# Two graph-attention layers in one kernel: the subtraction that forms the low half of the first layer's input, on GpSimd instead of VectorE from the eighth pair on

## The chip, the cores and the metric

One Trainium2 chip, one core of it. The metric is the device time of one execution in microseconds (us), the median over several runs. TensorE is called PE here, VectorE DVE, ScalarE ACT, GpSimd POOL, and SyncE, which issues all of the DMAs, SP. PEld is the loading of weights into PE, which overlaps the matmuls.

## The reference

The input is 64 graphs of 128 nodes with 256 features, `x` (64, 128, 256), and an integer adjacency `adj` (64, 128, 128). Two layers run one after the other.

```python
# layer 0
q, k, v = x @ Wq + bq, x @ Wk + bk, x @ Wv + bv        # 8 heads of 32
scores = einsum('bnhd,bmhd->bhnm', q, k) / sqrt(32); scores = where(adj == 0, -inf, scores)
h = einsum('bhnm,bmhd->bnhd', softmax(scores), v)
y = h @ Wo + bo + x;  x1 = layernorm(y) * gamma + beta
# layer 1, the same adj
q, k, v = x1 @ Wq.T + bq, ...;  p = softmax(where(adj == 0, -16384, q k^T)); z = v
for _ in range(4):
    z = 0.9 * (p @ z) + 0.1 * v
out = layernorm(x1 + z) * gamma + beta
```

## The kernel before, in words

The 64 graphs are worked on as 32 pairs. A pair's feature-major input is a tile of 128 partitions x 512 numbers (two chunks of 128 features, 2 x 128 nodes). The projections are made in three matmuls each instead of one: the input is split into a rounded copy `xh` and the rest `xl` (input minus rounded copy), the weights into `w_hi` and `w_lo`, and `xh·w_hi + xh·w_lo + xl·w_hi` is accumulated in PSUM (`project_T`, L338 to L345, and `project`, L347 to L353; the three products are `parts`, L324).

For the first layer the input comes by DMA into `xt_in` (two buffers, `load_xt`, L265). ACT rounds it into `xh[0]` (`split_hi`, L997; L1001), and DVE subtracts that from `xt_in` and writes `xl[0]` (`split_lo`, L1354; L1357). `xh[0]` and `xl[0]` have one buffer each. PE's `queries(0, ...)`, `keys(0, ...)` and `values(0, ...)` wait at their start for both counts, `xh_s` and `xl_s` (`x_ready`, L355 to L361), before the first of their matmuls, although `xl` is used only by the third product.

The order of the work is written out by hand. Each engine has its own list in three parts: `begin()` for the first pairs, `step(t)` for t = 7 to 31, and `end()`. A step works on many pairs at once, each at another stage. Engines run their lists strictly in order and meet at semaphores; a `Count` is a semaphore that rises by a fixed number per pair, so each wait names a pair.

What stands around the change in a step of each engine:

- DVE, `step` at L1688: the four `mask_scores(1, ...)` of pair t - 3, then `make_mask(t - 1)` (L1366), `split_lo(t)` (L1357), `save_ol(t - 2)` (L1423, which waits for ACT's `oh`), masked scores, `add_hop(1, ...)` (L1512), more masked scores, and `save_y(t - 2)` (L1439), the sum of the output projection and `xb`. At the step's head are `save_q(1)`, `add_hop(2, ...)` (L1512) and `reciprocals(0, 1, t - 2)` (L1409).
- POOL, `step` at L1981: `inverse_root(1, t - 8)` (L1872), `restart_term(t - 4)` (L1907, 0.1 v into `z0s`), `last_term(t - 4)` (L1914), `shift_residual(t - 3)` (L1899), `add_bias(t - 1)` (L1880, the row-major input plus a bias row, into `xb`; it waits for DVE's `save_y(t - 2)`), `inverse_root(0, t - 2)` (L1872), `probabilities` three times (L1859) with `scale_residual` (L1891) between them, `shift_out` (L1927), `scale_out` (L1921), and the last `probabilities`. `probabilities(0, 1, t - 1)` waits for DVE's reciprocals of that pair.
- PE, `step` at L671: for pair t - 1 it runs `queries(0, 0, t - 1)` (L699) behind the two `output` projections of pair t - 3, then values of the second layer, `queries(0, 1, t - 1)`, and so on. PE's step t + 1 is the one that uses what DVE's and POOL's step t make of pair t.
- SP, `step` at L312: `load_xt(t + 2)` waits for `xl_s` of pair t (L267), since the subtraction is the last reader of that `xt_in` buffer; then `store(t - 9)`, `load_x(t + 1)`, `load_adj(t + 2)`.

`begin()` on DVE holds `split_lo` of pairs 0 to 6; pairs 7 to 31 are split in `step`.

Of the kernel before, what the change touches and what calls it, by code (L numbers as in the profile page):

```python
# [6 lines left out]
FP32 = mybir.dt.float32  # L7
F32R = mybir.dt.float32r
I32 = mybir.dt.int32
ALU = mybir.AluOpType  # L10
# [69 lines left out]
def two_layers(nc, x, x_t, adj, w, rows, cols, ident_d, out):  # L80
    ctx = ExitStack()
    with ctx:
        def sb(name, shape, dt=FP32):
            return ctx.enter_context(nc.sbuf_tensor(name, shape, dt))
# [4 lines left out]
        def count(name, per=1):  # L89
            return Count(ctx.enter_context(nc.semaphore(name)), per)  # L90
# [30 lines left out]
        xt_in = [sb(f"xt_in{i}", [128, C, T]) for i in range(2)]  # L121
# [10 lines left out]
        xh = [sb(f"xh{l}", [128, C, T], F32R) for l in range(2)]  # L132
        xl = [sb(f"xl{l}", [128, C, T], F32R) for l in range(2)]
# [66 lines left out]
        xh_s = count("xh_saved")  # L200
        xl_s = count("xl_saved")
# [55 lines left out]
        def both(r):  # L257
            return r.broadcast_to([128, 2, D])
# [1075 lines left out]
        def _(dve):  # L1334
# [19 lines left out]
            def split_lo(p):  # L1354
                if p.real:
                    dve.wait_ge(xh_s.sem, xh_s.at(p))
                    nc.vector.tensor_tensor(xl[0][:, :, :], xt_in[p.parity][:, :, :], xh[0][:, :, :].bitcast(FP32),  # L1357
                                            ALU.subtract).then_inc(xl_s.sem, 1)
# [10 lines left out]
            def save_q(l, p):  # L1369
                if p.real:  # L1370
                    if p.is_(0):
                        dve.wait_ge(*((fold_s, 3) if l else (bq_s, 1)))
                    dve.wait_ge(qr[l].sem, qr[l].at(p))
                    dve.wait_ge(sr[l].sem, sr[l].at(p - 1))
                    raw = ps_q[l][:, :].rearrange("p (c t) -> p c t", c=C)
                    if l:
                        last = nc.vector.tensor_tensor(qT[l][:, :, :], raw, along(b1_col[:, 0, :]), ALU.add)
                    else:
                        last = nc.vector.scalar_tensor_tensor(out=qT[l][:, :, :], in0=raw, scalar=SCALE,
                                                              in1=along(bq0s[:, :]), op0=ALU.mult, op1=ALU.add)  # L1380
                    last.then_inc(q_s[l].sem, 1)

            def save_k(l, p):
                if p.real:
                    if l and p.is_(0):
                        dve.wait_ge(fold_s, 3)
                    dve.wait_ge(kr[l].sem, kr[l].at(p))
                    dve.wait_ge(sr[l].sem, sr[l].at(p - 1))
                    nc.vector.tensor_tensor(kT[l][:, :, :], ps_k[l][:, :].rearrange("p (c t) -> p c t", c=C),
                                            along(b1_col[:, 1, :] if l else col[:, BK0c, :]), ALU.add  # L1390
                                            ).then_inc(k_s[l].sem, 1)

            def mask_scores(l, b, c, p):
                if p.real:
                    dve.wait_ge(sr[l].sem, sr[l].at(p))
                    dve.wait_ge(mask_s.sem, mask_s.at(p))
                    dve.wait_ge(exps[l][b].sem, exps[l][b].at(p - 1))
                    for g in range(G):
                        h, o = G * c + g, 512 * g + (b * C + c) * N
                        last = nc.vector.tensor_tensor_reduce(  # L1400
                            sm[l][:, b, h, :], psS[:, o:o + N], mask[p.parity][:, b, :], -1.0, BIG,
                            ALU.add, ALU.min, nmax[l][:, b, h:h + 1])
                    last.then_inc(mx[l][b][c].sem, 1)

            def reciprocals(l, b, p):
                if p.real:
                    dve.wait_ge(exps[l][b].sem, exps[l][b].at(p))
                    dve.wait_ge(pr_s[l][b].sem, pr_s[l][b].at(p - 1))
                    nc.vector.reciprocal(rec[l][:, b, :], tot[l][:, b, :]).then_inc(rec_s[l][b].sem, 1)  # L1409
# [89 lines left out]
            def add_hop(j, p):  # L1499
                if p.real:  # L1500
                    dve.wait_ge(zr[j].sem, zr[j].at(p))
                    if j == NUM_HOP - 1:
                        dve.wait_ge(zf_s.sem, zf_s.at(p))
                        for used in on_s:
                            dve.wait_ge(used.sem, used.at(p - 2))
                        dst, add = y1[p.parity], zf[p.number % 4]
                    else:
                        if j == 0:
                            dve.wait_ge(z0_s.sem, z0_s.at(p))
                            dve.wait_ge(hr[NUM_HOP - 1].sem, hr[NUM_HOP - 1].at(p - 2))  # L1510
                        dst, add = z[p.parity], z0s[p.parity]
                    nc.vector.tensor_tensor(dst[:, :, :], ps_u[j][:, :].rearrange("p (b d) -> p b d", b=2), add[:, :, :],  # L1512
                                            ALU.add).then_inc(z_s[j].sem, 1)
# [174 lines left out]
            def step(t):  # L1688
                mask_scores(0, 1, 0, t - 2)
                save_q(1, t - 3)  # L1690
                add_hop(2, t - 6)
                reciprocals(0, 1, t - 2)
                save_k(1, t - 3)
                add_hop(0, t - 5)
                statistics(1, t - 7)
                mask_scores(1, 0, 0, t - 3)
                reciprocals(1, 1, t - 4)
                mask_scores(1, 1, 1, t - 3)
                mask_scores(1, 0, 1, t - 3)
                mask_scores(1, 1, 0, t - 3)  # L1700
                make_mask(t - 1)
                split_lo(t)
                save_ol(t - 2)
                mask_scores(0, 0, 1, t - 1)
                add_hop(1, t - 5)
                mask_scores(0, 0, 0, t - 1)
                save_y(t - 2)
                statistics(0, t - 2)
                aggregate(0, t - 2)
                save_q(0, t)  # L1710
                add_eps(0, t - 2)
                normalise(1, 0, t - 8)
                mask_scores(0, 1, 1, t - 1)
                normalise(0, 1, t - 2)
                normalise(0, 0, t - 2)
                reciprocals(1, 0, t - 3)
                normalise(1, 1, t - 8)
                save_k(0, t)
                aggregate(1, t - 7)
                add_hop(3, t - 6)  # L1720
                save_x1l(t - 2)
                save_hop(0, t - 4)
                reciprocals(0, 0, t - 1)
                add_eps(1, t - 7)
# [119 lines left out]

            begin()
            run(step, 7, PAIRS)
            end()

        @block.gpsimd
        def _(pool):  # L1850
# [12 lines left out]
            def inverse_root(l, p):  # L1863
                if p.real:
# [6 lines left out]
                            pool.wait_ge(used.sem, used.at(p - 1))  # L1871
                    nc.gpsimd.tensor_tensor(rstd[l][:, :], ve[l][:, :], mhalf[:, :], ALU.pow).then_inc(rstd_s[l].sem, 1)  # L1872

            def add_bias(p):
                if p.real:
                    if p.is_(0):
                        pool.wait_ge(fold_s, 1)
                    pool.wait_ge(x_s.sem(p), x_s.at(p))
                    pool.wait_ge(y_s.sem, y_s.at(p - 1))
                    nc.gpsimd.tensor_tensor(xb[:, :, :], x_in[p.parity][:, :, :], both(bo_row[:, :, :]), ALU.add  # L1880
                                            ).then_inc(xb_s.sem, 1)
# [12 lines left out]
            def shift_residual(p):  # L1894
                if p.real:
                    if p.is_(0):
                        pool.wait_ge(fold_s, 2)
                    pool.wait_ge(xg_s.sem, xg_s.at(p))
                    nc.gpsimd.tensor_tensor(zf[p.number % 4][:, :, :], zf[p.number % 4][:, :, :], both(r_row[:, :, :]), ALU.add  # L1899
                                            ).then_inc(xr_s.sem, 1)  # L1900
# [80 lines left out]
            def step(t):  # L1981
                inverse_root(1, t - 8)
                restart_term(t - 4)
                last_term(t - 4)
                shift_residual(t - 3)
                add_bias(t - 1)
                inverse_root(0, t - 2)
                probabilities(1, 0, t - 3)
                probabilities(0, 0, t - 1)
                scale_residual(t - 2)  # L1990
                probabilities(0, 1, t - 1)
                shift_out(t - 9)
                scale_out(t - 8)
                probabilities(1, 1, t - 3)
# [51 lines left out]

            begin()
            run(step, 7, PAIRS)
            end()

# [29 lines left out]
```

## Time and profile before

| what | us |
|---|---|
| median of 3 runs | 783.24 (782.63 to 788.65) |
| the profiled execution's own time | 786.14 |
| span of its trace | 784.0 |
| busy in the span: PE, PEld | 754.1, 710.6 |
| busy in the span: ACT, DVE, POOL | 665.7, 637.1, 547.8 |

The span runs from the first to the last instruction of the trace; the execution's own time has 2.1 us around it. From about 200 us to 659 us the trace repeats itself once per pair, every 22.96 us. A time in a row is the start from the beginning of the span; the next number is the duration. Consecutive instructions of one engine may overlap by a few hundredths of a us in the rows. In brackets stands how long the engine was idle just before and what ended that.

### The profile page before, as it was taken

What the parts mean: (1) busy time and instruction counts of PE and PEld (TensorE: products, weight loads), DVE (VectorE), ACT (ScalarE), POOL (GpSimd) and SP (SyncE); (2) the same over time, 40 slices, a digit from 0 to 9 for tenths busy, and PEclk for the clock granted to TensorE, in tenths of its full rate; (3) what the DMA queues carried; (4) which work ended last, traced back from release to release, by engine and by line L of the source; (5) the groups of instructions that cost most, each with busy time, mean ns of one, the idle gap of its engine ahead of it and who ended that gap; (6) DMA issues with size and microseconds to landing.
All of it is one profiled execution on the core that took longest, in us unless ns stands there. A gap on an engine that the chain in (4) does not pass through costs nothing.

```text
span 784.0 us, 32528 instructions
## 1 busy us (share of the span) xinstructions
PE 754.1 (96%) x11544; PEld 710.6 (91%) x11544; DVE 637.1 (81%) x3093; ACT 665.7 (85%) x2570; POOL 547.8 (70%) x417
## 2 busy tenths in 40 slices
PE   6889999999999999999999999999999999999974
PEld 6778999999999999999999999999999999998863
DVE  5778888888888888888888888888888888887765
ACT  4779998889889988988998898998889899899661
POOL 0336858666777777777787777787777778768774
PEclk9899999999999999999999999999999999999997
DMA  7101011010111101111111011111001111100002
GB/s 239 48 21 50 23 35 37 22 30 23 50 50 49 50 29 26 47 50 49 50 49 30 23 51 50 49 49 50 29 23 50 50 50 36 30 16 17 29 15 68
DMA packets 33245, 34.12 MB, mean 44 GB/s; under 512 B 2368, under 2 KB 28864, under 8 KB 33088
## 3 DMA queue, kind: packets, MB, share of 16 engines
q1 hardware_dynamic: 33088, 32.06, 13.8%
q8 instruction: 94, 1.54, 0.8%
q14 instruction: 63, 0.52, 0.2%
HBM read 23.67 MB, written 8.39 MB: 41 GB/s over the span
## 4 chain that ended last, share of the span: by engine, by line
PE 89%; DVE 3%; ACT 2%; issue 2%; DMA 1%; SPq 1%; POOL 1%; POOLq 0%; DVEq 0%; ACTq 0%
PE psF L342 23%; PE psF L411 18%; PE psF L351 16%; PE psF L401 15%; PE psS L391 9%; PE psF L456 7%; PE psF L436 2%; ACT ex L1011 2%; DMA w_raw<-in_w 1%; DVE sm L1400 1%; DMA out<-o_t 1%; SPq L284 0%; DVE o_t L1491 0%; DVE bst L1450 0%; POOL o_t L1927 0%
## 5 line engine op out<-in xcount | busy, mean ns | idle before, releaser
L1011 ACT ACTIVATE ex<-sm,nmax 128x128 f32<-128x128 f32 x1024 | 397.9, 397 | 3.3 <-DVE nmax L1400 2.3
L1859 POOL TENSOR_TENSOR pr<-ex,rec 128x1024 f32<-128x1024 f32 x128 | 245.3, 1918 | 101.1 <-DVE rec L1409 101.1
L1400 DVE CUSTOM_DVE_ANT_0 sm<-psS,mask 128x128 f32<-128x128 f32 x1024 | 228.3, 284 | 41.6 <-PE psS L391 41.4
L1011 ACT ACTIVATION_READ_ACCUMULATOR ex<-sm,nmax 128x1 f32 x1024 | 200.7, 196 | 0.0
L1022 ACT ACTIVATE pT<-psF 128x512 f32<-128x512 f32 x256 | 138.8, 596 | 34.5 <-PE psF L401 34.4
L401 PE MATMUL psF<-ident,pr 128*128 128x128 f32 x1024 | 137.8, 276 | 0.8 <-ACT pT L1022 0.5
L401 PEld LDWEIGHTS psF<-ident,pr 128*128 128x128 f32 x1024 | 112.7, 141 | 9.3 <-ACT pT L1022 0.9
L342 PE MATMUL psF<-xh,w_hi 128*128 128x256 f32 x512 | 112.6, 302 | 7.7 <-DVE w_lo L1339 5.7
L411 PE MATMUL psF<-pT,z 128*32 128x128 f32 x3072 | 103.1, 276 | 2.3 <-DVE z L1512 2.0
L342 PE MATMUL psF<-xh,w_lo 128*128 128x256 f32 x512 | 104.1, 285 | 0.0
L342 PE MATMUL psF<-xl,w_hi 128*128 128x256 f32 x512 | 103.6, 284 | 0.0
L342 PEld LDWEIGHTS psF<-xh,w_hi 128*128 128x128 f32 x512 | 79.8, 193 | 14.2 <-issue 12.6
L411 PEld LDWEIGHTS psF<-pT,z 128*32 128x32 f32 x3072 | 84.2, 111 | 8.1 <-issue 3.5
L1880 POOL TENSOR_TENSOR xb<-x_in,bo_row 128x512 f32<-128x512 f32 x32 | 41.7, 1302 | 70.2 <-DVE y L1439 52.9
L1400 DVE DVE_READ_ACCUMULATOR2_ANT nmax<- 128x1 f32 x1024 | 84.8, 83 | 0.0
L456 PE MATMUL psF<-ident,hT 128*128 128x128 f32 x512 | 76.4, 273 | 5.7 <-DVE hT L1416 3.9
L342 PEld LDWEIGHTS psF<-xh,w_lo 128*128 128x128 f32 x512 | 80.5, 193 | 0.0
L342 PEld LDWEIGHTS psF<-xl,w_hi 128*128 128x128 f32 x512 | 80.3, 192 | 0.0
L1872 POOL TENSOR_TENSOR rstd<-ve,mhalf 128x2 f32<-128x2 f32 x64 | 47.2, 737 | 43.5 <-DVE ve L1470 43.3
L391 PE MATMUL psS<-kT,qT 32*128 32x128 f32 x2048 | 75.3, 283 | 0.9 <-DVE nmax L1400 0.9
L391 PEld LDWEIGHTS psS<-kT,qT 32*128 32x128 f32 x2048 | 63.2, 186 | 11.8 <-issue 6.7
L1045 ACT ACTIVATE hT<-psF 128x512 f32<-128x512 f32 x96 | 57.0, 596 | 18.1 <-PE psF L411 18.0
(76 smaller groups left out, 1425.7 us busy)
## 6 DMA issues: line engine op xcount, KB each, us to landing
xt_in<-in_x_t SPq DMA_DIRECT2D x32, 256.0 KB, 3.0
x_in<-in_x SPq DMA_DIRECT2D x32, 256.0 KB, 3.0
out<-o_t SPq DMA_DIRECT2D x30, 256.0 KB, 2.2
adj_in<-in_adj SPq DMA_DIRECT2D x32, 128.0 KB, 2.4
pT<-in_w SPq DMA_DIRECT2D x4, 256.0 KB, 4.0
row<-in_rows SPq DMA_DIRECT2D x1, 768.0 KB, 6.8
w_raw<-in_w SPq DMA_DIRECT2D x3, 256.0 KB, 7.0
out<-o_t SPq DMA_DIRECT2D x4, 128.0 KB, 1.7
```

The lines of the kernel that those rows point to most:

```text
L342: last = nc.tensor.matmul(dst[:, c * T:(c + 1) * T], w_p[e][:, i, kc, c * 128:(c + 1) * 128], x_p[a][:, kc, :], start=(n == 0 and kc == 0) ...
L351: last = nc.tensor.matmul(dst[:, b * D:(b + 1) * D], x_p[a](kc), w_p[e][:, i, kc, :], start=(n == 0 and kc == 0), stop=(n == 2 and kc == C ...
L391: last = nc.tensor.matmul(psS[:, o:o + N], qT[l][r, c, b * N:(b + 1) * N], kT[l][r, c, b * N:(b + 1) * N], start=True, stop=True)
L401: last = nc.tensor.transpose(ps_T[l][b][c][:, g * N:(g + 1) * N], pr[l][:, b, G * c + g, :], ident[:, :])
L411: last = nc.tensor.matmul(dst[32 * g:32 * g + 32, o:o + N], src[:, b, h * HD:(h + 1) * HD], p_T[:, b, h, :], start=True, stop=True)
L456: last = nc.tensor.transpose(ps_u[j][:, o:o + 128], hT[p.parity][:, b * C + c, :], ident[:, :])
L1011: e = nc.scalar.activation(ex[l][:, b, h, :], sm[l][:, b, h, :], ACT.Exp, scale=-1.0, bias=nmax[l][:, b, h:h + 1], accum_out=tot[l][:, b, ...
L1022: nc.scalar.activation(pT[l][p.parity][:, b, G * c:G * c + G, :], ps_T[l][b][c][:, :].rearrange("p (g n) -> p g n", g=G), ACT.Copy).then_i ...
L1045: nc.scalar.activation(hT[p.parity][:, :, :], ps_h[j][:, :].rearrange("p (a n) -> p a n", n=N), ACT.Copy, scale=1.0 - ALPHA).then_inc(hT_s ...
L1400: last = nc.vector.tensor_tensor_reduce(sm[l][:, b, h, :], psS[:, o:o + N], mask[p.parity][:, b, :], -1.0, BIG, ALU.add, ALU.min, nmax[l][ ...
L1859: nc.gpsimd.tensor_tensor(pr[l][:, b, :, :], ex[l][:, b, :, :], rec[l][:, b, :].unsqueeze(2).broadcast_to([128, H, N]), ALU.mult).then_inc ...
L1872: nc.gpsimd.tensor_tensor(rstd[l][:, :], ve[l][:, :], mhalf[:, :], ALU.pow).then_inc(rstd_s[l].sem, 1)
```

## The change

From pair 7 on (the eighth), the subtraction `xt_in - xh` into `xl[0]` is no longer in DVE's step but in POOL's, between `shift_residual(t - 3)` and `add_bias(t - 1)`. Its operands, its shape, its waits and its count are the same; for pair 7 POOL also waits until DVE has done pair 6, so that the count stays in order. Pairs 0 to 6 stay on DVE. Nothing else is changed.

```diff
@@ DVE, step(t)
                 mask_scores(1, 0, 1, t - 3)
                 mask_scores(1, 1, 0, t - 3)
                 make_mask(t - 1)
-                split_lo(t)
                 save_ol(t - 2)
@@ POOL
+            def split_lo(p):
+                if p.real:
+                    pool.wait_ge(xh_s.sem, xh_s.at(p))
+                    if p.is_(7):
+                        pool.wait_ge(xl_s.sem, xl_s.at(p - 1))
+                    nc.gpsimd.tensor_tensor(xl[0][:, :, :], xt_in[p.parity][:, :, :], xh[0][:, :, :].bitcast(FP32),
+                                            ALU.subtract).then_inc(xl_s.sem, 1)
@@ POOL, step(t)
                 last_term(t - 4)
                 shift_residual(t - 3)
+                split_lo(t)
                 add_bias(t - 1)
                 inverse_root(0, t - 2)
```

## Rows read from the trace of the kernel before

**Rows 1.** The page, part 1: busy time, share of the span, instructions of each engine.
```profile
PE 754.1 (96%) x11544; PEld 710.6 (91%) x11544; DVE 637.1 (81%) x3093; ACT 665.7 (85%) x2570; POOL 547.8 (70%) x417
```

**Rows 2.** The page, part 4: the chain that ended last, shares by engine.
```profile
PE 89%; DVE 3%; ACT 2%; issue 2%; DMA 1%; SPq 1%; POOL 1%; POOLq 0%; DVEq 0%; ACTq 0%
```

**Rows 3.** Stretches of the span: length, busy time by engine, granted clock, DMA share, GB/s.
```profile
20.00:40.00 20.00, 16.80 (x162) 15.09 (x160) 15.80 (x58) 14.94 (x54) 8.07 (x6) 0.89 0.17 48
40.00:60.00 20.00, 18.07 (x212) 16.59 (x213) 14.13 (x83) 14.65 (x61) 7.04 (x6) 1.00 0.08 21
200.00:659.00 459.00, 459.00 (x7203) 437.48 (x7196) 384.50 (x1921) 411.02 (x1600) 344.44 (x261) 1.00 0.15 43
```

**Rows 4.** Timeline of DVE, pair 10: start us, duration us, engine, line, operation.
```profile
201.01 0.68 DVE L1357 TENSOR_TENSOR xl<-xt_in,xh 128x512 fp32r<-128x512 f32 x1
201.80 0.69 DVE L1423 TENSOR_TENSOR ol<-psF,oh 128x512 fp32r<-128x512 f32 x1
205.59 0.69 DVE L1439 TENSOR_TENSOR y<-psF,xb 128x512 f32<-128x512 f32 x1
```

**Rows 5.** Timeline of POOL, pair 10.
```profile
202.25 1.27 POOL L1914 TENSOR_TENSOR zf<-z0s,zf 128x512 f32<-128x512 f32 x1
203.49 1.28 POOL L1899 TENSOR_TENSOR zf<-zf,r_row 128x512 f32<-128x512 f32 x1
206.42 1.30 POOL L1880 TENSOR_TENSOR xb<-x_in,bo_row 128x512 f32<-128x512 f32 x1 [1.65 <-DVE y L1439]
```

**Rows 6.** Timeline of PE's weight loads: the first of queries(0, 0) for pair 10.
```profile
205.24 0.30 PEld L342 LDWEIGHTS psF<-xh,w_hi 128*128 128x128 f32 x2
```

**Rows 7.** Timeline of PE, DVE and POOL where POOL's next chain begins.
```profile
216.01 0.60 PE L456 MATMUL psF<-ident,hT 128*128 128x128 f32 x4
...
216.65 0.69 DVE L1512 TENSOR_TENSOR z<-psF,w_raw 128x512 f32<-128x512 f32 x1 [0.45 <-PE psF L456]
217.25 0.19 DVE L1409 RECIPROCAL rec<-tot 128x8 f32<-128x8 f32 x1
...
217.53 1.90 POOL L1859 TENSOR_TENSOR pr<-ex,rec 128x1024 f32<-128x1024 f32 x1 [0.26 <-DVE rec L1409]
```

**Rows 8.** Groups of POOL's instructions from 200 to 659 us: busy us, mean ns, idle before.
```profile
L1859 POOL TENSOR_TENSOR pr<-ex,rec 128x1024 f32<-128x1024 f32 x81 | 154.9, 1913 | 62.1 <-DVE rec L1409 62.1
L1907 POOL TENSOR_SCALAR z0s<-v 128x512 f32<-128x512 f32 x10 | 6.3, 632 | 0.8
```

**Rows 9.** Timeline of POOL, then of PEld: the same place for pair 30.
```profile
662.68 1.28 POOL L1899 TENSOR_TENSOR zf<-zf,r_row 128x512 f32<-128x512 f32 x1
...
664.44 0.30 PEld L342 LDWEIGHTS psF<-xh,w_hi 128*128 128x128 f32 x2
```

**Rows 10.** Timeline of POOL, DVE and PEld: the same place for pair 9.
```profile
178.66 1.59 POOL L1914 TENSOR_TENSOR zf<-w_raw,zf 128x512 f32<-128x512 f32 x1
180.21 1.29 POOL L1899 TENSOR_TENSOR zf<-zf,r_row 128x512 f32<-128x512 f32 x1
...
178.01 1.10 DVE L1357 TENSOR_TENSOR xl<-xt_in,xh 128x512 fp32r<-128x512 f32 x1
...
182.28 0.30 PEld L342 LDWEIGHTS psF<-xh,w_hi 128*128 128x128 f32 x2
```

**Rows 11.** Timeline of POOL and PEld: the same place for pair 7.
```profile
133.72 0.95 POOL L1907 TENSOR_SCALAR w_raw<-w_raw 128x512 f32<-128x512 f32 x1
135.99 1.31 POOL L1899 TENSOR_TENSOR zf<-zf,r_row 128x512 f32<-128x512 f32 x1
...
136.33 0.31 PEld L342 LDWEIGHTS psF<-xh,w_hi 128*128 128x128 f32 x2
```

**Rows 12.** Timeline of POOL and PEld: the same place for pair 31.
```profile
685.64 1.29 POOL L1899 TENSOR_TENSOR zf<-zf,r_row 128x512 f32<-128x512 f32 x1
...
688.84 0.30 PEld L342 LDWEIGHTS psF<-xh,w_hi 128*128 128x128 f32 x2
```

**Rows 13.** Timeline of SP's queue: the load of a later pair's input after pair 10's subtraction.
```profile
201.72 0.34 SPq L268 DMA_DIRECT2D xt_in<-in_x_t  x1
```

## The prediction

> **What bounds the kernel now.** I began with the page's busy shares. PE is busy 96% of the span, and even its weight loads fill 91%; ACT stands at 85%, DVE at 81%, POOL at 70% [rows 1]. The chain that ended last is PE to 89%, and POOL holds 1% of it [rows 2]. The table of stretches shows where the other 4% are: from 200 to 659 us PE is busy for 459.00 of 459.00 us at a granted clock of 1.00 of its 2.4 GHz level, so in the repeating part it waits for nobody, and the idle time lies in the opening and the ending [rows 3]. Two things follow. Work taken off DVE there can't shorten anything, because the engine that sets the period never waits for DVE. And whatever makes PE wait inside a period is added to that period in full, since PE has no gap in which to make it up. So the question is a single one: is the low half `xl` there when PE wants it? For that I laid the timelines of the four engines beside one another around one pair.
>
> **What is removed.** DVE's subtraction for pair 10 starts at 201.01 and takes 0.68, so `xl` is ready at 201.69 [rows 4]. PE's first weight load for that pair's queries is at 205.24 [rows 6]; the low half lies ready for 3.55 us. Taking 0.68 us off DVE brings DVE nothing: the next instruction, `ol`, starts at 201.80 and not at once, 0.11 us behind, because it waits for ACT's `oh` [rows 4], and at the head of the next step DVE waits 0.45 for PE before `z` [rows 7]. Gain: 0.
>
> **What is added.** One two-input instruction of 128x512 per pair on POOL, for pairs 7 to 31, 25 of them. The trace before has no such instruction on POOL with an fp32r output. Nearest rows: two inputs, the same shape, fp32 output, 1.27, 1.28 and 1.30 us [rows 5]. Bounds from further away: one input of that shape 0.632, two inputs of twice the size 1.913 [rows 8]. I take 1.28, the row of the same shape that sees the same neighbours. On DVE it was 0.68, so it is 0.60 longer; but that isn't the cost. The cost is where POOL's order puts it.
>
> POOL comes to it only after `shift_residual`, which starts at 203.49 and ends at 204.77 [rows 5]. POOL's instructions overlap by 0.03 (202.25 + 1.27 against 203.49), so the subtraction starts at 204.74 and ends at 206.02. PE must then be told. DVE to POOL takes 0.14 (`y` ends at 206.28, `xb` starts at 206.42 [rows 4, 5]) or 0.09 (`rec` ends at 217.44, `pr` starts at 217.53 [rows 7]); no row shows POOL to PE, so I take 0.10 and keep 0.05 to 0.20. `xl` counts for PE from 206.12, and PE wanted it at 205.24 [rows 6]. The queries wait for both halves before their first product, so no work in front covers this: **0.88 us of PE stall**.
>
> **Is the stall there in every period?** Only if POOL's chain does not come earlier as seen from PE once PE is late. The chain runs without a gap from `probabilities(0, 1)`. That one waited 0.26 for DVE's `rec`, which directly follows `z`, and `z` waited 0.45 for PE's transposes at 216.01 [rows 7]. Those transposes stand behind the queries in PE's list. So a late PE makes a late POOL chain, and the next pair finds the same 0.88. The period becomes 22.96 + 0.88 = 23.84. Pair 30 has the same distances as pair 10: `shift_residual` ends at 663.96, PE loads at 664.44, 0.48 later, against 205.24 - 204.77 = 0.47 [rows 5, 6, 9]. Pairs 10 to 30 are 21: 21 x 0.88 = **18.5**.
>
> **The first pairs and the last.** For pair 9 `shift_residual` ends at 181.50 and PE loads at 182.28, 0.78 later [rows 10]; pair 8 has the same distance. DVE's subtraction took 1.10 there and POOL's `last_term` beside it 1.59, against 0.68 and 1.27 for pair 10 [rows 4, 5, 10]. That collision goes with the change, so POOL is 0.32 earlier: `shift_residual` ends at 181.18, the subtraction at 181.18 - 0.03 + 1.28 = 182.43, and with 0.10 that is 182.53, a stall of 0.25; two pairs: **0.5**. Pair 7: `shift_residual` ends at 137.30, less 0.32 because `z0s`, which took 0.95 beside DVE's subtraction, goes back to 0.63: 136.98. The subtraction ends at 138.23, counts at 138.33, and PE wanted it at 136.33: **2.0** [rows 11]. Pair 31: `shift_residual` ends at 686.93, so `xl` counts at 688.28, and PE loads only at 688.84 [rows 12]: **0**.
>
> The collisions bear on a rule. The Trainium skill (SBUF — State Buffer, section "SBUF: two separate sides") says that DVE and POOL share a pair of ports as a lock, held for a whole instruction, and that a DVE instruction with two inputs in SBUF contends with a POOL one that reads SBUF. The trace agrees for pair 9 (1.10 and 1.59). By that rule alone the change takes away DVE's only such instruction of the repeating part, which speaks for it; but from pair 10 on DVE's 0.68 and POOL's 1.27 show nothing to win back, and the rule changes the sum by the 0.32 us already counted for the first pairs.
>
> **What moves on the queues.** `add_bias` stands behind the new instruction. It waits for `y`, ready at 206.28, and POOL is free at 206.02, so it still starts at 206.42: the 1.65 us in which POOL idled there hold the 1.28 [rows 5]. SP issues the next load into this `xt_in` buffer at 201.72 on DVE's count [rows 13], and will at about 206.1, 4.4 us later; that load is for two pairs on, two periods of 22.96 away, and nothing else of SP's becomes due before. Cost: 0. If that cover were gone it would be at most the 4.4 us once.
>
> **Sum.** 18.5 + 0.5 + 2.0 + 0 = 21.0 us. The profiled execution has 784.0 of span and 2.1 around it, 786.14, and would become 807.1. The median is 783.24, so I forecast 783.24 + 21.0 = **804.2**. Its own range: with 1.27 and 0.05 a period loses 0.82, 21 x 0.82 + 2.1 = 19.3; with 1.33 and 0.20 it loses 1.03, 21.6 + 2.6 = 24.2. With a microsecond for the medians: 801.5 to 808.5.
>
> **Rivals.**
>
> *Not slower: POOL's chain comes earlier.* If what releases POOL's `probabilities(0, 1)` were DVE's own work and not PE, then DVE, lighter by 0.68, and standing idle more while PE stalls, would hand over `rec` earlier as seen from PE, and the stall would die out after a pair or two. It decides at 0.88 us: that much earlier and nothing is lost, 783.2 to 785. For it: DVE is at 84% in the repeating part (384.50 of 459.00 [rows 3]). Against it: the 0.45 of waiting for PE right in front of `rec` [rows 7]. Chance 0.04. The Trainium skill (Perfetto Trace Analysis, section "Identifying the Most-Contended Engine") has the most occupied engine set the pace; by that alone an instruction moved between DVE and POOL, neither of them the fullest, leaves 783.2. It says nothing of order, and the 0.47 us between POOL and PE is a matter of order.
>
> *A cheap subtraction.* If POOL did it at the one-input price, 0.632, the stall would be 0.88 - 0.65 = 0.23 and pairs 8 and 9 would have none: 21 x 0.23 + 1.4 = 6.2, so 789.4, within 1% of before. Against it: every two-input row of this shape is at 1.27 or more. Chance 0.05.
>
> *A dear subtraction.* If the fp32r output or a collision brought it to the 1.913 of the double size, each of 24 stalls grows by 0.63: 21.0 + 24 x 0.63 = 36.1, so 819.3. A collision is possible: DVE runs `y`, with `xb` in SBUF and the other input in PSUM, from 205.59 [rows 4], inside the new instruction. Against it: no POOL row of the repeating part is stretched beside such DVE work. Chance 0.09.
>
> *The clock falls.* The granted clock was 0.89 from 20 to 40 us, where PE was busy 16.80 of 20, but 1.00 from 40 to 60 with 18.07 of 20 [rows 3]. The new period has PE idle for 0.88 of 23.84, 4%, far less than the 10% that kept 1.00. If it did fall to 0.89, the 522 us from 160 to 682 would take 65 us more, about 869. Chance 0.02.
>
> **How the numbers follow.** Forecast 0.80, dear 0.09, cheap 0.05, not slower 0.04, clock 0.02. Predicted 804.2. The range 797 to 812 holds the forecast's own and reaches half-way to the cheap and the dear case. One per cent, 7.8 us, is about what a measurement of this kernel can tell from no change. Within it lie the cheap case and nearly all of the not slower one: 0.08; faster by more than 1% 0.01, since PE has next to nothing to win; slower 0.91.
>
> **What would show it.** Right: POOL's `xl` of about 1.28 us directly behind `shift_residual`; PEld L342 now idle 0.6 to 1.0 us per pair, released by POOL's `xl`, about 20 us in all; a period of 23.8 us; `xb` still released by `y`; DVE's waits for PE longer; pair 7's stall near 2 us and pair 31's none; a granted clock of 1.00. Wrong: a period of 22.96 and no wait of PE on POOL; POOL's `probabilities(0, 1)` no longer waiting for `rec`; the new instruction far from 1.28; or PE waiting elsewhere in the period, on ACT or DVE.

## The result, and the profile after

| | before | changed |
|---|---|---|
| median of 4 runs each, us | 784.11 (782.63 to 788.65) | 805.43 (803.18 to 809.84) |
| the profiled execution, own time | 786.14 | 806.28 |
| its span | 784.0 | 803.7 |

The ratio is 1.0278, 95% interval 1.025 to 1.0307: 2.8% slower. The forecast was 804.2.

The page of the changed kernel, part 1 (busy time and shares, as in [rows 1]) and part 4 (the chain that ended last, as in [rows 2]):

```profile
PE 758.3 (94%) x11544; PEld 710.7 (88%) x11544; DVE 619.9 (77%) x3068; ACT 665.1 (83%) x2570; POOL 577.8 (72%) x442
...
PE 35%; POOL 34%; issue 22%; ACT 4%; DVE 3%; DMA 1%; POOLq 1%; SPq 0%; DVEq 0%; ACTq 0%
```

DVE is lighter by 17 us, POOL heavier by 30, and none of the engines is anywhere near full except PE. Yet POOL, which held 1% of the chain, holds 34%: it now leads from `rec` through POOL's instructions to `xl`, and from there through PE back to `rec`. That is the picture of an engine that is idle for more than a quarter of the time and nevertheless on the path.

The same place in the timelines as in [rows 5, 6], for pair 10 of the changed kernel; first POOL, then PE's weight loads:

```profile
203.55 1.27 POOL L1921 TENSOR_TENSOR zf<-z0s,zf 128x512 f32<-128x512 f32 x1
204.78 1.28 POOL L1906 TENSOR_TENSOR zf<-zf,r_row 128x512 f32<-128x512 f32 x1
206.03 1.28 POOL L1878 TENSOR_TENSOR xl<-xt_in,xh 128x512 fp32r<-128x512 f32 x1
207.73 1.30 POOL L1887 TENSOR_TENSOR xb<-x_in,bo_row 128x512 f32<-128x512 f32 x1 [0.42 <-DVE y L1439]
```
```profile
206.31 0.31 PEld L351 LDWEIGHTS psF<-w_hi,ol 128*128 128x128 f32 x2
207.42 0.30 PEld L342 LDWEIGHTS psF<-xh,w_hi 128*128 128x128 f32 x2 [0.81 <-issue]
...
207.46 0.47 PE L342 MATMUL psF<-xh,w_hi 128*128 128x256 f32 x2 [0.63 <-POOL xl L1878]
```

`xl` takes 1.28 and ends at 207.31, and PE's next weight load starts 0.11 later. It had been idle for 0.81. The bracket of the weight load names "issue", which is the profile's word for time in which it sees no wait; the matmul that follows names the releaser, POOL's `xl`. It does so for 22 of the 25 pairs: pair 7 and pairs 10 to 30. `xb` is still released by `y`; its idle time shrank from 1.65 to 0.42, so the added instruction did fit where POOL had been idle.

The head of POOL's next chain, against [rows 7], DVE and then POOL:

```profile
218.83 0.69 DVE L1512 TENSOR_TENSOR z<-psF,w_raw 128x512 f32<-128x512 f32 x1 [0.45 <-PE psF L456]
219.44 0.19 DVE L1409 RECIPROCAL rec<-tot 128x8 f32<-128x8 f32 x1
...
219.71 1.90 POOL L1858 TENSOR_TENSOR pr<-ex,rec 128x1024 f32<-128x1024 f32 x1 [0.26 <-DVE rec L1409]
```

The two waits, 0.45 and 0.26, are what they were to the hundredth. PE's delay travels through DVE into POOL, and the next pair meets the same stall. What DVE gave up became waiting: per pair it waits 0.7 for ACT's `oh` in front of `ol` (0.1 before), and 1.2 for PE's `queries(0, 0)` and `queries(0, 1)` in front of their `qT` (0.3 before). The first weight loads of `queries(0, 0)` of pairs 10 and 30 are at 207.42 and 684.72: 477.30 / 20 = 23.87 us per pair, against 22.96.

Here is where the time went, from the first weight load of `queries(0, 0)` of each pair in the two traces:

| from pair to pair | before, us | changed, us | more |
|---|---|---|---|
| 6 to 7 | 23.10 | 25.09 | 1.99 |
| 7 to 8 | 22.99 | 24.73 | 1.74 |
| 8 to 9 | 22.96 | 23.22 | 0.26 |
| 9 to 30 | 482.16 | 501.14 | 18.98 |
| 30 to 31 | 24.40 | 24.42 | 0.02 |
| together | 575.61 | 598.60 | 22.99 |

The spans differ by only 19.7, because the changed kernel's opening, up to pair 6, was 2.7 us shorter in its trace, and the ending 0.6. The opening isn't touched by the change: the profiled execution of before had a granted clock of 0.89 from 20 to 40 us [rows 3], and that of the changed kernel had 1.00. The experiments' traces have either, whatever the kernel (figures in the last section). The medians of several runs average over this, though with four runs each only roughly, and they say 21.3.

One line of that table isn't explained by a stall: from pair 7 to pair 8 PE waited for `xl` only 0.27 us (its weight loads idle for 0.19, and the usual overlap of 0.08 lost). The table of stretches of the changed kernel, columns as in [rows 3], shows the rest:

```profile
134.00:136.00 2.00, 0.34 (x3) 0.37 (x4) 1.57 (x5) 2.00 (x11) 2.00 (x3) 0.98 0.00 0
136.00:138.00 2.00, 2.00 (x12) 2.00 (x11) 0.00 (x0) 0.14 (x2) 0.76 (x1) 0.50 0.53 133
138.00:140.00 2.00, 2.00 (x14) 2.00 (x14) 0.42 (x1) 0.00 (x0) 0.00 (x0) 0.66 0.38 130
140.00:144.00 4.00, 4.00 (x43) 3.83 (x45) 2.97 (x17) 2.90 (x9) 2.60 (x2) 1.00 0.02 4
...
206.00:683.00 477.00, 464.19 (x7199) 439.15 (x7199) 372.45 (x1901) 410.79 (x1599) 369.05 (x281) 1.00 0.14 41
```

Right after pair 7's wait (PE busy 0.34 of 2 us) the granted clock is 0.50 and then 0.66 of 2.4 GHz. That is the 1.2 GHz level for all of the one stretch and two thirds of the other, some 3.4 us. PE's first matmul behind the wait, two rows inside that time and two behind it, each of two matmuls:

```profile
135.66 0.53 PE L342 MATMUL psF<-xh,w_hi 128*128 128x256 f32 x2 [1.85 <-POOL xl L1878]
...
136.42 0.63 PE L342 MATMUL psF<-xl,w_hi 128*128 128x256 f32 x2
136.84 0.63 PE L351 MATMUL psF<-w_hi,xh 128*128 128x256 f32 x2
...
139.38 0.40 PE L351 MATMUL psF<-w_hi,xh 128*128 128x256 f32 x2
139.62 0.40 PE L351 MATMUL psF<-w_lo,xh 128*128 128x256 f32 x2
```

Two take 0.43 from start to start there (0.42 in these two rows), and 0.24 at the full clock; over 3.4 us that is a loss of 3.4 x (1 - 0.24 / 0.43) = 1.5. With pair 8's own stall of 0.27 it gives the 1.74 of the table. The stalls of 0.9 us from pair 10 on are followed by nothing of the kind: 1.00 throughout. This is one profiled execution. Of the other three of the changed kernel one, the 803.18, had a mean granted clock of 0.994 against the 0.992 of this one, so the fall may not come in every execution; no trace shows one without it.

### The profile page after: what moved, and what is told of

Same layout as the page of the kernel before. It is cut to its first block, busy times and chain, and to the rows that moved or that the text cites. A ratio compares the mean times of both kernels' runs of the same rounds, so it can differ in the third digit from the quotient of the medians.

```text
span 803.7 us, 32529 instructions
## 1 busy us (share of the span) xinstructions
PE 758.3 (94%) x11544; PEld 710.7 (88%) x11544; DVE 619.9 (77%) x3068; ACT 665.1 (83%) x2570; POOL 577.8 (72%) x442
## 4 chain that ended last, share of the span: by engine, by line
PE 35%; POOL 34%; issue 22%; ACT 4%; DVE 3%; DMA 1%; POOLq 1%; SPq 0%; DVEq 0%; ACTq 0%
POOL pr L1858 11%; PE psF L342 11%; PE psF L351 8%; PE psF L401 6%; PE psF L411 5%; POOL zf L1921 4%; POOL o_t L1934 4%; POOL zf L1898 4%; POOL zf L1906 4%; POOL xl L1878 3%; PE psS L391 2%; ACT ex L1011 2%; POOL rstd L1871 2%; PE psF L456 2%; POOL o_t L1928 1%
```

## The experiments

The intervals are those of the ratio to the kernel before, which was run again beside each group of experiments (medians 783.15 to 784.09). "Period" is the time from pair to pair between 200 and 660 us in the profile.

| kernel | median, us | ratio | period, us |
|---|---|---|---|
| changed | 805.43 | 1.0278 (1.025 to 1.0307) | 23.87 |
| xl one place earlier on POOL | 784.47 | 1.0003 (0.998 to 1.0026) | 22.96 |
| xl at the head of POOL's step | 782.65 | 0.9982 (0.9958 to 1.0005) | 22.96 |
| xl behind xb on POOL | 923.83 | 1.1789 (1.1751 to 1.1827) | 28.0 to 29.5 |
| extra work on POOL | 783.87 | 0.9994 (0.9971 to 1.0018) | 22.96 |
| no low half | 781.96 | 0.9975 (0.9957 to 0.9993) | 22.96 |
| PE waits at the third product | 792.74 | 1.0119 (1.0088 to 1.015) | 23.33 |
| POOL from pair 9 | 801.93 | 1.0232 (1.0202 to 1.0262) | 23.85 |
| late on DVE | 813.40 | 1.0383 (1.0341 to 1.0425) | 24.13 |
| PE's values first | 787.77 | 1.0032 (1.0006 to 1.0058) | 23.08 |

### The place in POOL's list: one earlier, three earlier, one later

```diff
 # POOL, step(t), from the changed kernel: one place earlier
                 last_term(t - 4)
+                split_lo(t)
                 shift_residual(t - 3)
-                split_lo(t)
                 add_bias(t - 1)
```

> The subtraction stays on POOL but stands one place earlier, in front of shift_residual instead of behind it. Theory A (place): the price is only how late xl is for PE. xl then ends about 1.25 us earlier, near 204.8 on the scale of pair 10, and PE wants it at 205.24, so no stall from pair 8 on and some 0.7 us once for pair 7: 784.5 to 786, a period of 22.96. Rival B (load): an engine of which 1.3 us per pair more is asked, or POOL being the slower engine for it, costs the time wherever it stands: 803 to 806.

It came out at 784.47, not distinguishable from before. POOL and PEld for pair 10:

```profile
203.41 1.30 POOL L1878 TENSOR_TENSOR xl<-xt_in,xh 128x512 fp32r<-128x512 f32 x1
204.66 1.31 POOL L1906 TENSOR_TENSOR zf<-zf,r_row 128x512 f32<-128x512 f32 x1
...
205.17 0.30 PEld L342 LDWEIGHTS psF<-xh,w_hi 128*128 128x128 f32 x2
```

`xl` ends at 204.71, 0.46 before PE loads, and nobody waits. Two neighbouring lines exchanged in one engine's list are worth 21 us. Pair 7 still stalled once, by 0.8 (23.87 from pair 6, against 23.10).

```diff
 # POOL, step(t), from the changed kernel: at the head
                 inverse_root(1, t - 8)
+                split_lo(t)
                 restart_term(t - 4)
                 last_term(t - 4)
                 shift_residual(t - 3)
-                split_lo(t)
                 add_bias(t - 1)
```

> The subtraction on POOL stands directly behind inverse_root(1), in front of restart_term. A: xl ends near 202.8, 2.4 us before PE wants it; shift_residual ends near 206.05, still before xb's wait for y ends at 206.42. No stall, pair 7 included: 783.5 to 785. B: 803 to 806. A third outcome, 786 to 790, would mean that the terms now 1.3 us later (z0s, last_term) are missed by DVE's last hop.

782.65: a little below the forecast, its interval holds 1. POOL and PEld for pair 10:

```profile
198.64 1.28 POOL L1878 TENSOR_TENSOR xl<-xt_in,xh 128x512 fp32r<-128x512 f32 x1
...
202.46 0.30 PEld L342 LDWEIGHTS psF<-xh,w_hi 128*128 128x128 f32 x2
```

`xl` ends at 199.92 and PE loads at 202.46; pair 7 has no stall either (22.99). `z0s`, `last_term` and `shift_residual`, each 1.3 us later, are missed by nobody.

```diff
 # POOL, step(t), from the changed kernel: behind add_bias
                 shift_residual(t - 3)
-                split_lo(t)
                 add_bias(t - 1)
+                split_lo(t)
```

> The subtraction on POOL stands behind add_bias instead of in front of it. A: xb ends at 207.72, xl at 208.97, PE gets it at about 209.1, 3.9 us after 205.24: 24 x 3.9 + 3 for pair 31 = 97, so 881 if the granted clock stays at 1.00. If each stall of that length is followed by 3.4 us at half clock, as the one of 2.03 us of pair 7 was, 1.7 us more per pair: about 922. B: 803 to 806.

923.83, near the larger of theory A's two figures. POOL, PEld for pair 10, and the stretch from 206 to 659 us (columns as in [rows 3]):

```profile
220.67 1.27 POOL L1887 TENSOR_TENSOR xb<-x_in,bo_row 128x512 f32<-128x512 f32 x1 [1.66 <-DVE y L1439]
221.90 1.26 POOL L1878 TENSOR_TENSOR xl<-xt_in,xh 128x512 fp32r<-128x512 f32 x1
...
223.28 0.50 PEld L342 LDWEIGHTS psF<-xh,w_hi 128*128 128x128 f32 x2 [3.72 <-issue]
...
206.00:659.00 453.00, 396.34 (x5662) 376.61 (x5661) 293.19 (x1499) 324.17 (x1263) 291.63 (x223) 0.91 0.12 35
```

PE stood still for 3.72 us in every pair. Those stalls would make a period of 22.96 + 3.8 = 26.8; the mean from pair 7 to pair 30 is (796.58 - 137.71) / 23 = 28.65. The 1.9 us beyond it are the clock: 0.91 on average where it was 1.00, and the weight load behind the wait takes 0.50 for two where it took 0.30. Once per period the trace has a stretch at the 1.2 GHz level, of 3.4 or 6.8 us. From the first weight load of pair 7 to that of pair 30 these add up to 109.3 us, of which 10.4 lie inside the waits and cost nothing more. The other 98.9 are 4.3 per pair, and at the rate of the changed kernel 4.3 x (1 - 0.24 / 0.43) = 1.9. That the 922 was met so closely is partly luck: it was worked out with 3.4 us per pair at half speed, 1.7.

### Is it the load, or the engine?

```diff
 # from the kernel before: DVE keeps its subtraction, POOL does one more, for t = 7 to 31
                 shift_residual(t - 3)
+                extra(t)      # scratch = row[:, 0:2, :] - row[:, 2:4, :], 128x512, fp32r
                 add_bias(t - 1)
```

> DVE keeps its subtraction as in the kernel before; POOL does an additional one of the same shape from constant tiles into a tile that nobody reads, at the place of the change, pairs 7 to 31. A: it fits into the 1.65 us in which POOL waits for y, nobody waits for it: 783.5 to 785.5, period 22.96. B (POOL's 1.3 us of additional work is what costs): 803 to 806.

783.87. POOL's rows at that place:

```profile
202.22 1.31 POOL L1879 TENSOR_TENSOR scratch<-row 128x512 fp32r<-128x512 f32 x1
203.91 1.30 POOL L1888 TENSOR_TENSOR xb<-x_in,bo_row 128x512 f32<-128x512 f32 x1 [0.38 <-DVE y L1441]
```

The same instruction at the same place, with nobody waiting for it, is free. Work on POOL is not what costs.

```diff
 # from the kernel before, DVE, step(t)
                 make_mask(t - 1)
-                split_lo(t)
                 save_ol(t - 2)
                 mask_scores(0, 0, 1, t - 1)
                 add_hop(1, t - 5)
                 mask_scores(0, 0, 0, t - 1)
+                split_lo(t)
                 save_y(t - 2)
```

> The subtraction stays on DVE but stands directly in front of save_y instead of in front of save_ol. A (only lateness counts, not the engine): it would end at 206.27 on the scale of pair 10, PE gets it 1.1 us after 205.24, period 24.1, 24 pairs x 1.1 = 26: 809 to 813. Rival D (it is the move to POOL that costs, by the slower engine or the shared ports): 783 to 786.

813.40, slower than the changed kernel, although nothing moved to POOL and the subtraction took 0.69. DVE and PEld for pair 10:

```profile
206.56 0.69 DVE L1357 TENSOR_TENSOR xl<-xt_in,xh 128x512 fp32r<-128x512 f32 x1
...
207.36 0.30 PEld L342 LDWEIGHTS psF<-xh,w_hi 128*128 128x128 f32 x2 [1.08 <-issue]
```

On the faster engine, but done later, it costs more: the period is 24.13, 1.17 over before. The median is 0.4 above the top of what was expected; the period grew by 1.17 and not by 1.1, which makes 24 x 0.07 = 1.7. With that, and with the two places on POOL that cost nothing, the rival that blames the engine or the shared ports is out.

### What could have been won

```diff
 # from the kernel before: no split_lo from pair 7 on
 # DVE, step(t)
                 make_mask(t - 1)
-                split_lo(t)
                 save_ol(t - 2)
 # PE, x_ready (layer 0)
-                    pe.wait_ge(xl_s.sem, xl_s.at(p))
+                    if p.number < 7:
+                        pe.wait_ge(xl_s.sem, xl_s.at(p))
 # SP, load_xt waits for xh_s instead of xl_s where pair p - 2 is 7 or later
```

> Left out: the low half of the first layer's input for pairs 7 to 31 (nobody computes it, PE reads the one of pair 6 and does not wait for it; the load of xt_in is released by the rounded copy). DVE is lighter by 0.68 us per pair and POOL as before. It measures the most that could have been won by taking the subtraction off DVE. A: nothing, PE has no gap: 782.5 to 785, period 22.96. Rival C (DVE's 0.68 us per pair are on the path): 767 to 780.

781.96; the ratio is 0.9975, its interval just below 1. The period is 22.96, PE is busy for every microsecond of the repeating part:

```profile
206.00:659.00 453.00, 453.00 (x7127) 431.65 (x7125) 367.62 (x1878) 405.28 (x1574) 340.51 (x257) 1.00 0.15 42
```

So even with the subtraction gone altogether the kernel gains 0.25%, and none of it in the repeating part. No placing of it can be expected to bring more.

### The reader's side

```diff
 # from the changed kernel, PE, project_T for queries(0, 0) alone
+                    if n == 2:
+                        pe.wait_ge(xl_s.sem, xl_s.at(p))      # in front of xl·w_hi; xh is waited for in front of all
```

> The changed kernel, but queries(0, 0) waits for xh before its first product and for xl only before its third. A: the four matmuls of the first two products, 0.47 us from 205.24 to 205.71 in the weight loads, go under the wait; the stall of 0.90 per pair becomes 0.43, the period 23.4: 21 x 0.43 + 1.5 for pair 7 = 10.5 us over before, 794 to 797. B: 803 to 806.

792.74, a little below the expected band. POOL and the weight loads for pair 10:

```profile
203.56 1.31 POOL L1884 TENSOR_TENSOR xl<-xt_in,xh 128x512 fp32r<-128x512 f32 x1
...
204.08 0.30 PEld L344 LDWEIGHTS psF<-xh,w_hi 128*128 128x128 f32 x2
204.32 0.31 PEld L344 LDWEIGHTS psF<-xh,w_lo 128*128 128x128 f32 x2
204.92 0.30 PEld L344 LDWEIGHTS psF<-xl,w_hi 128*128 128x128 f32 x2 [0.30 <-POOL xl L1884]
```

Without the wait the third pair of loads would come at 204.55; it comes at 204.92: a stall of 0.37, not 0.43. The 0.47 of covered work went as expected; the other 0.06 is in the hand-over, which takes 0.05 here (`xl` ended at 204.87) and 0.11 in the changed kernel. Pair 7 lost 1.5 here (24.53 from pair 7 to pair 8, against 22.99), its weight loads idle for 1.50, without a fall of the clock.

```diff
 # from the changed kernel, PE, step(t)
-                free((z_s[1], t - 6))
-                queries(0, 0, t - 1)
                 free((hT_s[3], t - 7))
                 values(1, 0, t - 4)
-                queries(0, 1, t - 1)
                 values(1, 1, t - 4)
+                free((z_s[1], t - 6))
+                queries(0, 0, t - 1)
+                queries(0, 1, t - 1)
```

> The changed kernel, DVE and POOL untouched, but PE's step runs both values(1, .) of pair t - 4 in front of queries(0, 0) and queries(0, 1) of pair t - 1 instead of between them. Twelve matmuls, 1.42 us, then stand in front of the wait for xl. Theory A (xl is late by 0.90 only as measured against the place of the queries in PE's list): the stall goes, period 22.96, some 0.6 us for pair 7: 784 to 787. Rival B (POOL's work costs as such): 803 to 806. A third outcome, 788 to 800, would mean that the queries, 0.7 us later, or what hangs on them (qT, the second layer's values on the same banks) becomes the next wait.

787.77, between theory A's band and that of the third outcome: the stall is gone, as A says, and a small new cost is there, as the third outcome says. POOL and PEld for pair 10, then DVE:

```profile
206.33 1.30 POOL L1878 TENSOR_TENSOR xl<-xt_in,xh 128x512 fp32r<-128x512 f32 x1
...
208.28 0.30 PEld L342 LDWEIGHTS psF<-xh,w_hi 128*128 128x128 f32 x2
...
210.00 0.69 DVE L1379 SCALAR_TENSOR_TENSOR qT<-psF,bq0s 128x512 f32<-128x512 f32 x1 [1.06 <-PE psF L342]
```

`xl` ends at 207.63 and PE wants it at 208.28. The period is 23.08, 0.12 too long. In PE's list the third group of four transposes behind the queries waits for `qT`, which ends at 210.69; the twelve weight loads for the transposes begin at 209.70 and come every 0.11 up to the eighth at 210.46, so the ninth, the first of the third group, would come at 210.57. It comes at 210.74, 0.05 behind `qT`. The stretches show the gap (busy times of PE, PEld, DVE, ACT and POOL):

```profile
210.46:210.60 0.14, 0.14 (x4) 0.14 (x2) 0.14 (x1) 0.14 (x1) 0.00 (x0) 1.00 0.00 0
210.60:210.74 0.14, 0.14 (x3) 0.00 (x0) 0.14 (x3) 0.14 (x1) 0.00 (x0) 1.00 0.00 0
```

The ninth is 0.17 late, and the tenth follows after 0.06 instead of 0.11: 0.12 are left, the size of the loss. That is read off the trace; it was not tried by itself.

### Pair 7 and the clock

```diff
 # from the changed kernel
 # DVE, step(t)
                 make_mask(t - 1)
+                if t.number < 9:
+                    split_lo(t)
                 save_ol(t - 2)
 # POOL, step(t); the wait for the last pair on DVE is at pair 9
-                split_lo(t)
+                if t.number >= 9:
+                    split_lo(t)
```

> The changed kernel, but POOL takes over at pair 9; DVE does pairs 7 and 8 as well. In the changed kernel the profile shows for pair 7 a stall of 2.03 us, followed at once by 3.4 us of PE at half the granted clock, which cost another 1.7. If that stall is pair 7's own (POOL late from begin()) and the half clock follows from it, neither is there: about 4 us less than the changed kernel, 800.5 to 802.5, granted clock 1.00 from 40 to 700 us. If the first pair on POOL always costs it: as the changed kernel, 804 to 806.

801.93, 3.5 below the changed kernel's median. The runs of the two kernels were not made side by side, so the difference of two ratios, 1.0278 against 1.0232, is the better measure: 0.46% of 784, 3.6 us; the intervals overlap slightly. The trace is clear where the medians alone aren't:

```profile
131.00:160.00 29.00, 29.00 (x468) 27.53 (x461) 25.31 (x117) 26.36 (x104) 20.61 (x17) 1.00 0.13 39
```

No stall at pair 7 (23.12 from pair 6), no fall of the clock, and pair 9 as POOL's first costs 0.27.

## Why the prediction was right

**What bounds the kernel.** Said: PE waits for nobody in the repeating part, so what DVE gives up is worth 0 and every wait of PE counts in full. The kernel without the low half has the period of before, 22.96, to the hundredth; its 0.25% lies outside. This step held.

**The lateness.** Said: `xl` takes 1.28 behind `shift_residual` and is 0.88 late. Measured: 1.297 in the median of 25 (mean 1.294), and 0.90 per pair ((501.14 - 482.16) / 21 = 0.904). The term of 18.5 for pairs 10 to 30 was 19.0. The missing 0.02 per pair is POOL's, whose `xl` takes up to 1.32, and the hand-over to PE, assumed at 0.10, measured at 0.11.

**That it doesn't die out.** Said: the head of POOL's chain hangs on PE through `z` and `rec`. Both waits were unchanged, and the 21 periods are 23.84 to 23.87 long. The rival in which DVE's lighter load pulls POOL forward had 0.04 and did not happen; DVE does wait longer for PE, as forecast, in front of `qT`.

**The first pairs.** Pair 7: 2.0 forecast, 1.99 found. Pairs 8 and 9: 0.25 each forecast, 0.27 and 0.26 found. The 0.32 for the vanished collision was right as well. Pair 9 in the changed kernel:

```profile
179.70 1.27 POOL L1921 TENSOR_TENSOR zf<-w_raw,zf 128x512 f32<-128x512 f32 x1
180.93 1.28 POOL L1906 TENSOR_TENSOR zf<-zf,r_row 128x512 f32<-128x512 f32 x1
```

`last_term` is back from 1.59 [rows 10] to 1.27. So the rule of the Trainium skill (SBUF — State Buffer, section "SBUF: two separate sides"), by which DVE and POOL hold shared ports as a lock, agrees with the trace in that the two stretched each other and no longer do, and the effect had the small size that the rows had given it. That one of them is blocked for the whole of the other's instruction is not shown: in [rows 10] the two overlap by 0.45 (178.66 to 179.11), and `last_term` is longer by 0.32.

**The last pair and the queues.** Pair 31 without a stall: 24.42 against 24.40. The instruction hidden in front of `y`, and the load of `xt_in`, now issued at 207.34, right behind `xl`, instead of 201.72, were put at 0 each: nothing was seen of them.

**What was missed.** The sum was 21.0; from pair 6 to pair 31 the traces show 23.0. Of the 2.0 between them, 0.5 are the 0.02 per pair, and 1.5 are the fall of the clock behind pair 7's wait. The step that failed is the one that dealt with the clock: it judged by PE's idle share over a long stretch (4% against 10%) and for the repeating stall only. For that it held, at 1.00. It never asked what the single wait of 2.0 us at pair 7, which the prediction itself forecasts further up, would do. That the medians, 21.3 apart, lie so near the 21.0 is therefore in part luck: four runs of one kernel scatter by 6 us and would not show 1.5. The traces and the kernel that starts at pair 9 do.

**The rule on occupancy** (the Trainium skill, Perfetto Trace Analysis, section "Identifying the Most-Contended Engine") would have left 783.2 for the changed kernel. In the runs it answers one half of the question: the most occupied engine, PE, did bound the period, and nothing taken from DVE moved it. It doesn't see that POOL at 72% can hold PE up by being late.

**The price of the subtraction.** The dear and the cheap one are settled by the 1.297 us.

## What to carry to other kernels

Before work is moved to an engine "with room", compare two times in one trace: when the instruction would end at its new place in that engine's list, and when the reader wants the result; busy shares give neither. If the bounding engine has no gaps and the late engine's chain starts from something that engine produces, the lateness is paid again in every period, and exchanging two neighbouring lines can be worth all of it (784.5 against 805.4 here). Price a rare long wait of PE separately from the frequent short ones, for the clock behind it may fall (1.5 us behind the 2.0 here).

## What the runs showed of the hardware that was not expected

The granted clock of PE fell with some waits and not with others. It stayed at 1.00 with PE's weight loads idle 0.82 us in every pair (the changed kernel), with 1.08 in every pair and 1.34 once (late on DVE), and with 1.50 once (the wait at the third product), each in the middle of otherwise gapless work; it went to the 1.2 GHz level for 3.4 us behind the single 2.03 (the changed kernel), and for 3.4 or 6.8 us in every period with 3.72 in every pair (behind xb), 0.91 on average. In the last case the period was 1.9 us longer than the waits alone make it, and the fall began inside the wait in some periods and just behind it in others. These are the lengths that occurred; where between them it changes, and whether length alone decides, no run here tells.

In the opening the clock fell in some executions and not in others of kernels whose opening is all but the same: 0.89 from 20 to 40 us in the profiled execution of before, 1.00 in that of the changed kernel. Without a fall the first weight load of `queries(0, 0)` of pair 6 comes at 110.5 to 111.3 us (seven traces), with 3.4 us at the lower level at 112.4 and 112.5 (one place earlier, from pair 9), with 6.8 us at 113.2 (before). What decides which it is, no run shows. The 2.7 us between before and the changed kernel are as much as three of the forecast's stalls, and they are a reason to read such effects from the periods and not from one total.
